# The first expert layer of a four-layer transformer stack: from every expert on every token to tokens sorted by expert through DRAM

## What is computed

```python
x = hidden_states.reshape(-1, c)                      # layer-normalised, 2048 x 128
logits = (x @ w_red) @ wg_n.T                         # 8 experts
gates = softmax(logits, axis=1)
scores = max(gates, axis=1); idx = argmax(gates, axis=1)
h = einsum('nc,ech->neh', x, W1) + b1[None]           # 128 -> 256, per expert
h = gelu(h[token, idx[token]])
o = einsum('nh,ehc->nec', h, W2) + b2[None]           # 256 -> 128
o = o[token, idx[token]] * scores[:, None]
x = x + o
```

## Time and profile before

| | us |
|---|---|
| three runs | 399.02, 404.8, 426.97 |
| median of the runs | 404.8 |
| the profiled execution, first to last instruction | 400.2 |
| TensorE busy in it | 355.2 |
| VectorE busy | 252.4 |
| ScalarE busy | 189.4 |
| GpSimd busy | 165.3 |

### The profile page before, as it was taken

The page is one execution under the profiler, slowest core; times in us unless marked ns, Lnnn a source line. Parts: engine busy times, 40 slices in busy tenths (PEclk is TensorE's granted clock), DMA queues, the critical chain, the costliest instruction groups (busy, mean ns, idle before and its releaser), DMA issues.

```text
span 400.2 us, 5681 instructions
## 1 busy us (share of the span) xinstructions
PE 355.2 (89%) x1871; PEld 276.1 (69%) x1875; DVE 252.4 (63%) x608; ACT 189.4 (47%) x316; POOL 165.3 (41%) x161
## 2 busy tenths in 40 slices
PE   0885999999999999999889967797849999999995
PEld 0673778877787788777466756574528878878883
DVE  4445526644564454863799999979974665665652
ACT  1525524662546364545455533474424445444452
POOL 5539302100210151432385631736743555555553
PEclk9988699999999999999999998999978999999998
DMA  7604000000000000000000000000000000000000
GB/s 264 247 1 162 7 2 1 2 0 2 1 1 2 2 0 2 1 2 1 0 2 1 2 0 0 2 1 1 0 0 2 27 2 0 26 0 0 26 0 26
DMA packets 2408, 8.14 MB, mean 20 GB/s; under 512 B 432, under 2 KB 544, under 8 KB 2000
## 3 DMA queue, kind: packets, MB, share of 16 engines
q1 hardware_dynamic: 1984, 6.49, 4.4%
q10 hardware_dynamic: 400, 1.34, 1.0%
HBM read 6.78 MB, written 1.05 MB: 20 GB/s over the span
## 4 chain that ended last, share of the span: by engine, by line
PE 62%; DVE 22%; issue 9%; ACT 2%; DMA 2%; POOL 1%; POOLq 0%; another core or an unknown queue 0%; SPq 0%; ACTq 0%; DVEq 0%
PE bank L1112 58%; DVE xn L808 3%; DVE sc L944 3%; DVE mx L937 2%; PE bank L1124 2%; DMA pack_a<-in_pack_a 2%; DVE act L1073 1%; DVE z L949 1%; DVE st L797 1%; PE bank L1299 1%; DVE bqrep L878 1%; DVE rz L953 1%; PE bank L1163 1%; DVE route L972 1%; POOL an L738 1%
## 5 line engine op out<-in xcount | busy, mean ns | idle before, releaser
L759 POOL TENSOR_TENSOR w1l<-hm,w1h 128x512 fp32r<-128x512 f32 x48 | 62.2, 1298 | 41.8 <-ACT w1h L604 41.6
L913 DVE TENSOR_TENSOR hm<-act,bank 128x512 f32<-128x512 f32 x64 | 43.3, 685 | 52.3 <-ACT act L520 51.6
L1112 PEld LDWEIGHTS bank<-w,hm 128*128 128x128 f32 x512 | 65.6, 195 | 10.1 <-issue 5.1
L1112 PE MATMUL bank<-w,hm 128*128 128x128 f32 x512 | 71.8, 286 | 0.1
L520 ACT ACTIVATE act<-bank,pack_b 128x512 f32<-128x512 f32 x64 | 43.4, 687 | 56.6 <-PE bank L1112 55.9
L1073 DVE TENSOR_TENSOR act<-act,bank 128x512 f32<-128x512 f32 x48 | 33.0, 687 | 38.9 <-ACT act L619 38.7
L619 ACT ACTIVATE act<-bank 128x512 f32<-128x512 f32 x48 | 28.7, 598 | 51.8 <-PE bank L1112 51.5
L663 POOL TENSOR_SCALAR ve<-mv 128x4 f32<-128x4 f32 x16 | 3.7, 228 | 113.0 <-DVE mv L801 109.0
L1112 PE MATMUL bank<-xTh,gu1h 128*128 (+3 forms) x104 | 43.5, 418 | 2.4 <-DVE act L1073 2.4
L1112 PE MATMUL bank<-xTh,gu1l 128*128 (+3 forms) x104 | 41.8, 402 | 0.0
L1112 PE MATMUL bank<-xTl,gu1h 128*128 (+3 forms) x104 | 41.6, 400 | 0.0
(11 more groups left out here) (198 smaller groups left out, 671.5 us busy)
## 6 DMA issues: line engine op xcount, KB each, us to landing
wf<-in_gu SPq DMA_DIRECT2D x1, 1632.0 KB, 7.2
x<-in_x SPq DMA_DIRECT2D x4, 256.0 KB, 9.3
wf<-in_w ACTq DMA_DIRECT2D x1, 1024.0 KB, 6.6
w<-in_w SPq DMA_DIRECT2D x1, 1024.0 KB, 11.4
out_x<-x SPq DMA_DIRECT2D x4, 256.0 KB, 2.0
w<-in_w SPq DMA_DIRECT2D x1, 768.0 KB, 12.7
pack_a<-in_pack_a SPq DMA_DIRECT2D x1, 455.0 KB, 6.0
pack_b<-in_pack_b SPq DMA_DIRECT2D x1, 360.0 KB, 8.4
```

The lines of the kernel that those rows point to most:

```text
L759: nc.gpsimd.tensor_tensor(hml_slot(r)[0:m], hm_slot(r)[0:m], hmh_slot(r)[0:m].bitcast(F32), ALU.subtract).then_inc(s.hml_ready, 1)
L913: nc.vector.tensor_tensor(hm[:, r % 4, :], act[:, r % 4, :], bank[2 + r // 2 % 2][:, :], ALU.mult).then_inc(s.hm_ready, 1)
L1112: return nc.tensor.matmul(dst, lhsT, rhs, start=start, stop=stop, skip_group_check=True)
```

## The change

The expert layer is computed only for the tokens that chose the expert. The steps are:

- The first attention and router run for all four chunks ahead of the expert layer, as eight stages (`stage0`) with a new chunk every second step (`STEPS0`, 14 steps). The stages are: 0 statistics; 1 normalise, transpose, scores; 2 shift and exp; 3 softmax, transposes and output products; 4 addition to x and statistics; 5 normalise, transpose, logits; 6 one-hot and ranks; 7 rows and scatter. In a step the chunks stand in order, so PE's list in step 7 is stage 5 of chunk 1, stage 3 of chunk 2, stage 1 of chunk 3. Layer norm's normalisation goes from DVE to ACT everywhere, and POOL's `rstd_of` has four operations for two.
- The router writes a one-hot matrix `oh16` in bfloat16. PE counts with small products how many tokens of each expert stand ahead of each token, and so gives each token a row (`slot0`) in its expert's region of a DRAM buffer `xs_dram`. POOL writes the normalised tokens there with one indirect DMA per tile (`scatter`, 16 in all, 128 rows of 512 bytes each). SP pads the ends of the regions with zeros.
- DVE works out a table of 23 row tiles (`T0` = 16 + 8 - 1): which expert and which row each begins at. SP reads the table into registers, four tiles at a time.
- The rows are computed in 23 tiles of 128. For each, SP loads one expert's weights (128 partitions of 642 floats, 321 KB) and 128 rows of tokens (64 KB) into one of four slots (`SLOTS0`); PE transposes, multiplies with the two halves of the first layer and of the second; ACT does the Gelu for each half; DVE copies the transposed tokens and adds the bias. SP stores the result of tile u - 4 to `ys_dram` just ahead of the loads for tile u, in its own order of instructions.
- When all results are stored, POOL fetches each token's row back (`fetch`, indirect, 8 tiles ahead of the second attention and 8 in its loop), and DVE multiplies by the gate's score and adds to x (`combine`).
- What shared the rounds of the dense layer moves: the rounding of the last layer's weights (`round_gu`, `round_w2`) to ACT ahead of the tiles, their low halves to DVE between the tiles' steps; the second attention's block matrices from POOL to DVE ahead of the tiles; the second attention's norms, transposes and queries for chunks 0 to 2 into its loop (`ahead`), the first chunk's ahead of it.
- `gu1` is loaded at the start, since it has a buffer of its own; the loads of `w1`, `w2_0` and `sel0` go away.

The core of the diff:

```diff
+STAGES0, LAG0 = 8, 2
+STEPS0 = [[(s - LAG0 * c, c) for c in range(B) if 0 <= s - LAG0 * c < STAGES0] for s in range(STAGES0 + LAG0 * (B - 1))]
...
+T0 = NT + E0 - 1
+T0PAD = 24
+HID0 = R0 // E0
+SLOTS0 = 4
+W0_COLS = 2 * HID0 * P + HID0 + C
+PIECES = 8
...
+            def load_weights(t, e):
+                sp.dma_start(wb[:, t % SLOTS0, :], a["w0"][bass.ds(e, 1)].rearrange("o p n -> (o p) n"))\
+                    .then_inc(s.ld_wb[t % SLOTS0], 16)
+            def store_tokens(t):
+                sp.wait_ge(s.y0_ready, t + 1)
+                sp.dma_start(ys_dram[t * P:(t + 1) * P, :], ys[:, t % SLOTS0, :]).then_inc(s.kept_y[t % SLOTS0], 16)
+            def load_tokens(t, row):
+                sp.dma_start(xs[:, t % SLOTS0, :], xs_dram[bass.ds(row, P), :]).then_inc(s.ld_xs[t % SLOTS0], 16)
+            sp.wait_ge(s.zero_ready, 1)
+            sp.dma_start(xs_dram[E0 * REGION:E0 * REGION + (E0 - 1) * P, :].rearrange("(n p) c -> p n c", p=P),
+                         zeros[:, :].unsqueeze(1).broadcast_to([P, E0 - 1, C])).then_inc(s.padded, 16)
+            sp.wait_ge(s.ends_ready, 1)
+            _, ends = nc.values_load_multi_w_load_instructions(
+                tile_z[0:1, :], engines=(mybir.EngineType.SP,), min_val=0, max_val=E0 * REGION - P)
+            for e in range(E0):
+                sp.dma_start(xs_dram[bass.ds(ends[e], P), :], zeros[:, :]).then_inc(s.padded, 16)
+            sp.wait_ge(s.table_ready, 2)
+            for t in range(0, T0, SLOTS0):
+                own = range(t, min(t + SLOTS0, T0))
+                _, experts = nc.values_load_multi_w_load_instructions(
+                    tile_e[0:1, t:min(t + SLOTS0, T0)], engines=(mybir.EngineType.SP,), min_val=0, max_val=E0 - 1)
+                _, first = nc.values_load_multi_w_load_instructions(
+                    tile_r[0:1, t:min(t + SLOTS0, T0)], engines=(mybir.EngineType.SP,), min_val=0, max_val=(E0 + 1) * REGION - P)
+                for u in own:
+                    if u >= SLOTS0:
+                        store_tokens(u - SLOTS0)
+                    load_weights(u, experts[u - t])
+                    if u == 0:
+                        sp.wait_ge(s.scattered, 16 * NT)
+                        sp.wait_ge(s.padded, 16 * (E0 + 1))
+                    load_tokens(u, first[u - t])
+            for t in range(T0 - SLOTS0, T0):
+                store_tokens(t)
...
+            for t in range(T0):
+                act_e.wait_ge(s.h0_mm, t + 1)
+                if t >= 2:
+                    act_e.wait_ge(s.y0_mm, t - 1)
+                for k in range(HID0):
+                    last = nc.scalar.activation(hT0[:, t % 2, k, :], bank[2 + t % 2][:, k * P:(k + 1) * P], ACT.Gelu,
+                                                bias=b0_1[:, t % SLOTS0, k:k + 1])
+                last.then_inc(s.h0_ready, 1)
...
+            def scatter(c):
+                pool.wait_ge(s.slot_ready, c + 1)
+                for t in range(c * TPB, (c + 1) * TPB):
+                    nc.gpsimd.indirect_dma_start(xs_dram[:, :], bass.IndirectOffsetOnAxis(ap=slot0[:, t:t + 1], axis=0),
+                                                 xn2[:, t, :], None).then_inc(s.scattered, 16)
+            def fetch(t):
+                nc.gpsimd.indirect_dma_start(xn2[:, t, :], None, ys_dram[:, :],
+                                             bass.IndirectOffsetOnAxis(ap=home0[:, t:t + 1], axis=0)).then_inc(s.fetched[t // TPB], 16)
...
+            pool.wait_ge(s.home_ready, 1)
+            for i in range(SLOTS0):
+                pool.wait_ge(s.kept_y[i], 16 * len(range(i, T0, SLOTS0)))
+            for t in range(2 * TPB):
+                fetch(t)
+            rstd_of(2, 0)
             for i in range(NT + 4):
                 if 1 <= i <= NT:
...
+                for b in ahead(i, FETCH3):
+                    rstd_of(2, b)
+                if i + 2 * TPB < NT:
+                    fetch(i + 2 * TPB)
                 for b in starts(i, ADD):
                     rstd_of(3, b)
                 for b in looped(i, T4):
-                    low_half(3, b)
-                if i % 2 == 0 and 1 <= i // 2 <= 5:
...
+                elif k == 7:
+                    v.wait_ge(s.ex0_ready, c + 1)
+                    step(nc.vector.tensor_reduce(z0[:, c, :], lt0[:, c, :, :], AX, ALU.add))
+                    nc.vector.reciprocal(tiles(score0, c), z0[:, c, :])
+                    v.wait_ge(s.rank_mm, c + 1)
+                    step(nc.vector.tensor_tensor(rk0[:, c, :, :], ranks_of(c), tiles(oh16, c), ALU.mult))
+                    step(nc.vector.tensor_reduce(z0[:, c, :], rk0[:, c, :, :], AX, ALU.add))
+                    nc.vector.tensor_copy(tiles(slot0, c), z0[:, c, :]).then_inc(s.slot_ready, 1)
...
+            nc.vector.tensor_tensor(tile_z[:, :], bank[6][0:1, 2 * P:2 * P + E0], base_f[0:1, 0:E0], ALU.add)\
+                .then_inc(s.ends_ready, 1)
+            step(nc.vector.tensor_tensor(over0[:, :, :], bank[6][0:1, 2 * P:2 * P + E0].unsqueeze(2).broadcast_to([1, E0, NT]),
+                                         tab_thr.unsqueeze(1).broadcast_to([1, E0, NT]), ALU.is_gt))
...
+            for t in range(T0 + 2):
+                if t < T0:
+                    v.wait_ge(s.xs_mm, t + 1)
+                    if t >= 2:
+                        v.wait_ge(s.h0_mm, t - 1)
+                    nc.vector.tensor_copy(xsT[:, t % 2, :], bank[t % 2][:, 0:P]).then_inc(s.xsT_ready, 1)
+                if t < PIECES:
+                    low_gu(t)
+                elif t < PIECES + 5:
+                    low_w2(t - PIECES)
+                elif t < PIECES + 5 + B:
+                    b = t - PIECES - 5
+                    nc.vector.tensor_scalar(maskrow[:, b, :, :], rows_of(mask8[:, b * KV:(b + 1) * KV], H1), -BIG / P, None,
+                                            ALU.mult).then_inc(s.mask_ready, 1)
+                if t >= 2:
+                    u = t - 2
+                    v.wait_ge(s.y0_mm, u + 1)
+                    if u >= SLOTS0:
+                        v.wait_ge(s.kept_y[u % SLOTS0], rounds0(u - SLOTS0))
+                    nc.vector.tensor_tensor(ys[:, u % SLOTS0, :], bank[4 + u % 2][:, 0:C], b0_2[:, u % SLOTS0, :],
+                                            ALU.add).then_inc(s.y0_ready, 1)
+            def combine(b):
+                v.wait_ge(s.fetched[b], 16 * TPB)
+                for t in range(b * TPB, (b + 1) * TPB):
+                    last = nc.vector.scalar_tensor_tensor(x[:, t, :], xn2[:, t, :], score0[:, t:t + 1], x[:, t, :], ALU.mult, ALU.add)
+                last.then_inc(s.x2_ready, 1)
+                v.wait_ge(s.x2_ready, b + 1)
...
                 if 1 <= i <= NT:
                     total(i - 1)
-                if 1 <= i < NT:
+                if i < NT:
                     shift(i)
                 if 1 <= i <= NT:
                     inverse(i - 1)
-                if i == LN3:
-                    statistics(2, B - 1)
-                if i == NORM3:
-                    normalise(2, B - 1)
+                for b in ahead(i, FETCH3):
+                    combine(b)
...
+            for t in range(T0 + 2):
+                if t < T0:
+                    pe.wait_ge(s.ld_xs[t % SLOTS0], rounds0(t))
+                    if t == 0:
+                        pe.wait_ge(s.home_ready, 1)
+                    elif t >= 2:
+                        pe.wait_ge(s.xsT_ready, t - 1)
+                    nc.tensor.transpose(bank[t % 2][:, 0:P], xs[:, t % SLOTS0, :], ident).then_inc(s.xs_mm, 1)
+                if 1 <= t <= T0:
+                    u = t - 1
+                    pe.wait_ge(s.ld_wb[u % SLOTS0], rounds0(u))
+                    pe.wait_ge(s.xsT_ready, u + 1)
+                    if u >= 2:
+                        pe.wait_ge(s.h0_ready, u - 1)
+                    for k in range(HID0):
+                        last = mm(bank[2 + u % 2][:, k * P:(k + 1) * P], w0_1[:, u % SLOTS0, k, :], xsT[:, u % 2, :])
+                    last.then_inc(s.h0_mm, 1)
+                if t >= 2:
+                    u = t - 2
+                    pe.wait_ge(s.h0_ready, u + 1)
+                    if u >= 2:
+                        pe.wait_ge(s.y0_ready, u - 1)
+                    for k in range(HID0):
+                        last = mm(bank[4 + u % 2][:, 0:C], hT0[:, u % 2, k, :], w0_2[:, u % SLOTS0, k, :],
+                                  start=(k == 0), stop=(k == HID0 - 1))
+                    last.then_inc(s.y0_mm, 1)
...
+                if i < NT:
                     scores(i)
                 if 3 <= i < NT + 3:
                     attn_transposes(i - 3)
                 if i >= 4:
                     attn_values(i - 4)
-                if i == T3:
-                    transposes(2, B - 1, 6)
-                if i == QUERY:
-                    queries(B - 1)
+                for b in ahead(i, T3):
+                    transposes(2, b, 6)
+                for b in ahead(i, QUERY):
+                    queries(b)
```

(2 more changed lines are left out.)

973 lines of the change are left out of this document (468 added, 505 removed).

## The result

The changed kernel takes 422.24 us (median of four runs, 419.51 to 423.88), the kernel before in the same measurement 402.97 (four runs, 399.02 to 426.97). The ratio is 1.050, with a 95% interval of 1.042 to 1.059: slower by 5%, where 377 was forecast. The profiled execution spans 419.9 us. (The run of before at 426.97 was disturbed and is left out of the ratio.)

What follows compares the result with a forecast made beforehand. PE was taken to bound the kernel until 194 us, with DVE setting the pace behind it. From 400.2 us, 21.1 came off at the second attention's first `maxima` and 2 behind it: 377, range 358 to 402.

Steps and rivals of the forecast that it cites:

- The front's period, 11.9 us: PE's list per chunk before the tiles: stage 5 2.6, stage 3 4.1, stage 4 and start of 5 5.2 us.
- a period over 14: Sign against the forecast: PE's front list taking over 14 us a chunk.
- The clock: In the tiles, PE's low clock adds 0.7 us per two iterations, 7 us in all, inside the range.
- the joint: From the eighth fetch issued at 164.1 us to the second attention's first `maxima` at 171.8.
- Table, moved constants, first tile: Between router and tiles: last rows known at 67 us, table at 71, tile 0 at 81, range 72 to 90.
- The ring, 3.15 us an iteration: Row tiles: two iterations take loads 3.6 plus compute 2.1 us; registers add 0.3 a tile; range 2.5 to 4.2.
- The fetches, 1.2 us each: POOL's eight indirect fetches ahead of the second attention take 9.6 us, to 164.1.
- The second rival: POOL's indirect DMAs cost 2.4 us each: +9.6 us ahead of the mark, about +7 in the loop; 393 us, chance 0.14.
- Behind the mark, net -2: Second attention's loop onward: DVE work -4.2 us, POOL's fetches and next chunk's chain +2.2; range -6 to +8.
- the mark: The second attention's first `maxima`, at 192.89 us before, forecast at 171.8, a gain of 21.1.
- the slow ring: In the tiles, the tokens' round trip replaces PE as the bound: 5.1 us an iteration, 414 us, chance 0.12.
- a spacing over 4.4: Sign against the forecast: the tiles' Gelu pairs over 4.4 us apart, where 3.15 was expected.

Runs made afterwards that it cites:

- Experiments 3 and 4: Changed kernel with the first attention's output products grouped by weight height, 411.85 us (second form); changed kernel with unread products in PE's front waits, 411.98 us.
- experiment 9: Changed kernel with five slots, registers by the tile, grouped output products, earlier loop fetches and normalisations, and unread products: 377.23 us; without the unread products 384.29 us.
- experiment 5: Changed kernel plus unread products, four in each tile iteration and seventy behind the last tile: 415.08 us.
- experiments 1 and 2: Changed kernel with five slots for row tiles in place of four, 412.58 us; changed kernel with three slots, 481.28 us in one run.
- Experiment 8: Changed kernel with all sixteen fetches ahead of the second attention's loop and later chunks' normalisation steps started earlier: 406.75 us.

## Why the prediction was wrong, by its steps

**The front's period, 11.9 us: mis-sized, and the first cause.** Measured 16.55. By its three terms: stage 5 was put at 2.6 and takes 3.5 (46.03 to 49.55), stage 3 at 4.1 and takes 6.7 (49.55 to 56.28), the rest at 5.2 and takes 6.3 (to 62.58). Three periods give 14.0 too many, and a start 3.9 us later (transposes at 29.4 instead of 25.5, since the normalisation ends at 27.72 + 1.63) the rest of the 17.4 (behind the last start 0.4 us less are needed than forecast). The prediction named the order of PE's list as the bound, which was right, and it named "a period over 14" as what would prove it wrong. What failed is the price: it called the 3.4 us of the sixteen output instructions the slow rate, while they were alternating instructions at the full clock, and it took the front to run at the clock of the rows that it summed. Experiments 3 and 4 take mainly one cause each: 10.7 us for the grouping, 11.1 for the clock; they overlap, since the grouping also raised the clock in places. Both together (experiment 9) bring the last rows to 68.05, 16.4 us earlier, and leave 1.1 of the 17.4 for any other cause.

**The clock.** The prediction priced the low level at 7 us, for the tiles only. There it was 3 to 5, with 2.5 more in the joint (experiment 5). In the front, which it did not price, it was 11. In the earlier trace rows the granted clock was 0.53 from 45 to 50 us although PE was busy there; that row was read as a detail, and it was the warning. In the kernel before the low level filled the first microseconds and three short stretches between 23 and 50 us, and from 60 to 240 us the clock was full. In the changed kernel it filled nearly all of the front and the joint and most of the tiles (0.56 from 104.5 to 172 us).

**Table, moved constants, first tile: right.** From the last rows to the first tile 15.4 us against 14, with what it named: block products and home operations on DVE, ended at 99.64, with the first weights' load at 95.56 beside them.

**The ring, 3.15 us an iteration: right.** Results every 3.08 us, 72.5 us for the phase against 71, and in it PE waits 27.9 us, in 18 places, for the DMA of tokens. The round trip bound by the slots is shown by experiments 1 and 2. The share of the registers was put at 1.2 us a group; alone they take 2.9, part of which the ring's wait hides. Two iterations late in the ring, where no registers stand in between, from one result over the load that it releases to the result of that iteration:

```profile
163.74 0.29 DVE L1031 TENSOR_TENSOR ys<-bank,wb 128x128 f32<-128x128 f32 x1 [1.42 <-PE bank L1211]
165.09 0.33 SPq L509 DMA_DIRECT2D xs<-sorted_x  x1
167.81 0.48 PE L1336 MATMUL bank<-pack_a,xs 128*128 128x128 f32 x1 [1.79 <-DMA xs<-sorted_x]
170.03 0.29 DVE L1031 TENSOR_TENSOR ys<-bank,wb 128x128 f32<-128x128 f32 x1 [1.42 <-PE bank L1211]
```

That is 1.35 us to the issue and 2.72 to the landing, 4.1 where 3.6 was forecast, then 2.2 where 2.1 was: 6.3 against 5.7. The forecast's 0.3 a tile for registers made up for a loading that it had put too low, so the sum is better than its terms. The Trainium skill (DMA: Bandwidth & Descriptors, Anatomy of one DMA) puts one DMA at about 2.0 us plus its bytes, and it gives this for DMAs that GpSimd issues, while these are SP's. The rule would give estimates of 2.9 us for the tokens behind their weights and of 2.2 for a store; the medians of 23 were 2.8 and 1.5, so this trace agrees for the loads, and its stores are quicker.

**The fetches, 1.2 us each: right.** The issue takes 0.94 to 1.02 us and the next follows 1.25 after; the last of eight ends 9.8 us after the first begins, against 9.6. The second rival (2.4 each) is refuted. By the Trainium skill (SBUF — State Buffer, SBUF: two separate sides) GpSimd cannot write a DMA's descriptors while VectorE holds the shared port. The fetches in the loop, with DVE at work beside them, would show it; all sixteen have a mean of 984 ns, the first eight, with DVE mostly idle, 953. That is 0.06 us more a fetch for the later eight, too little to matter here. Which of VectorE's operations beside them held the port, the trace does not tell, so this shows only that the sharing cost little in this kernel.

**The joint, 7.7 us: mis-sized.** It takes 11.1: ACT's four normalisations 1.65 instead of 1.1, the query 2.07 instead of 1.02, scores 2.04 instead of 1.02, transposes 1.09 instead of 0.66. PE's three are the clock again (experiment 5 gives back 2.5).

**Behind the mark, net -2: the second cause, and a wrong mechanism.** It is +16.7 against before. The prediction weighed what DVE loses and gains and gave +2.2 to the chain of the next chunk that "must fit in four steps". It does not fit. The gain on DVE is there, but DVE is no longer what sets the pace: it works 14.01 of the 20 us from 200 to 220, where it worked 19.90. In the kernel before the chains of chunks 0 to 2 lay under the dense rounds (`early`), the cover that the change removes; the prediction named this loss for the moved constants, where it was small, and not for these three chains. By the start times the chain's parts after are sum 1.13, statistics 1.25, POOL 1.9, normalisation 1.6, transposes 1.1, copy 0.6, query 1.3 to 2.1, its copy 0.7, with scores behind them: some 11 us with the waits between. It is started four steps ahead, and in the kernel before the first four steps took 2.0 us each and the fifteen 2.9 in the mean; this happens three times, where before had one such chain in the loop. Experiment 8 shows it: 12.7 of the 18.6 us come back by order alone, with the clock that the shorter waits hold up. What the remaining 5.9 are made of was not tried.

**The rivals.** None of them is what happened, though the slow ring's 414 lies near the result. That rival was to be told by a spacing over 4.4, and the spacing is 3.08. A time that agrees with a rival's doesn't show its mechanism.

## What to carry to other kernels

When a change thins out an engine's work, two things go that no row of the old profile has as a cost: the clock that the dense work held up, and the cover under which other chains ran. List every step that ran beside the removed work and price its whole chain at the low clock, as if nothing lay beside it. Price a row only after you know at which clock level it ran and in which order: where the clock column has no record yet, a duration of the same shape elsewhere in the trace tells the level. And a change that comes out slower may be a faster design whose neighbours are not yet ordered for it: here 422 us became 384 by another order of the same work and one more slot, and 377 with products that nobody reads, against 399 for the best of the old design that was tried.
